# Four chained residual blocks on one core: adapter halves in fp16 turned by DMA, inner rows in one product, stacked low-rank product

## What is computed

```
x += attention with 16 heads: queries from f, keys and values from x, one own key and value per query from f,
     a length mask (always all-true here), projections Wq, Wk, Wv, Wo
x += softmax((x + stage embedding) @ f^T) @ f
x += layernorm(h + relu(h @ W1 + b1) @ W2 + b2) * gamma + beta     with h = x; W1 512x128, W2 128x512 of the batch's language
x += (x @ A^T) @ B^T + lang_embed                                  with A 16x512, B 512x16 of the batch's second language
```

## Time and profile before

| | us |
|---|---|
| median of 3 runs | 1315.94 (1315.02 to 1317.57) |
| the profiled execution: its time, its span | 1315.8, 1314.0 |
| PE busy | 1254.3 |
| DVE busy, ACT busy, POOL busy | 855.0, 849.9, 488.6 |
| one middle (batch 2 to 3), start to the next attention | 87.73 |

### The profile page before, as it was taken

The page is one execution under the profiler, slowest core; times in us unless marked ns, Lnnn a source line. Parts: engine busy times, 40 slices in busy tenths (PEclk is TensorE's granted clock), DMA queues, the critical chain, the costliest instruction groups (busy, mean ns, idle before and its releaser), DMA issues.

```text
span 1314.0 us, 19231 instructions
## 1 busy us (share of the span) xinstructions
PE 1254.3 (95%) x6697; PEld 519.7 (40%) x6697; DVE 855.0 (65%) x1553; ACT 849.9 (65%) x1803; POOL 488.6 (37%) x428
## 2 busy tenths in 40 slices
PE   7889999999999999999999999999999999999995
PEld 4332454325543345323543245431454324533252
DVE  5876449764596547964379643887439854497544
ACT  4898339873598636975379753888429883498631
POOL 6414363143731246321562416514254143631114
PEclk9999999999999999999999999999999999999997
DMA  6303532135223153132521334213343036222010
GB/s 217 69 13 107 113 65 65 54 97 103 57 57 92 64 97 73 41 123 51 91 61 49 115 73 81 63 44 107 89 78 74 19 107 121 57 65 68 25 33 32
DMA packets 156142, 98.85 MB, mean 75 GB/s; under 512 B 107338, under 2 KB 130182, under 8 KB 156046
## 3 DMA queue, kind: packets, MB, share of 16 engines
q1 hardware_dynamic: 155984, 97.61, 30.5%
q10 hardware_dynamic: 62, 0.01, 0.0%
HBM read 40.81 MB, written 8.40 MB: 37 GB/s over the span
## 4 chain that ended last, share of the span: by engine, by line
PE 66%; DVE 17%; ACT 14%; issue 2%; POOL 1%; ACTq 0%; POOLq 0%
PE bank L469 24%; PE banks L469 13%; DVE nmx L1086 10%; ACT big L858 7%; PE bank L1444 7%; PE banks L1428 6%; ACT banks L807 4%; PE banks L1363 4%; PE bank L1265 2%; PE bank L1391 2%; PE bank L1396 2%; PE bank L1418 2%; PE bank L1454 1%; DVE x L1147 1%; DVE big L1143 1%
## 5 line engine op out<-in xcount | busy, mean ns | idle before, releaser
L807 ACT ACTIVATE banks<-banks,nmx 128x512 f32<-128x512 f32 x512 | 342.4, 687 | 28.4 <-DVE nmx L1086 26.2
L1086 DVE TENSOR_REDUCE nmx<-banks 128x1 f32<-128x512 f32 x512 | 329.5, 685 | 35.8 <-PE banks L1363 34.7
L858 ACT ACTIVATE big<-banks 128x1024 f32<-128x1024 f32 x256 | 247.2, 1022 | 44.1 <-PE banks L1428 43.1
L469 PE MATMUL bank<-fT,w_hi 128*128 128x512 f16 x768 | 256.7, 380 | 0.7 <-DVE fT L1000 0.6
L1363 PE MATMUL banks<-KQ 97*128 97x512 f16 x512 | 196.5, 384 | 16.9 <-ACT banks L807 15.8
L1428 PE MATMUL banks<-KQ 98*128 98x512 f16 x512 | 141.0, 382 | 13.6 <-ACT big L858 8.7
L469 PE MATMUL bank<-fT,w_lo 128*128 128x512 f16 x384 | 145.9, 380 | 0.0
L504 POOL TENSOR_TENSOR split<-tiles_in,ones 128x512 f16<-128x512 f32 x56 | 60.3, 1078 | 223.5 <-DMA xT<-split 208.6
L504 POOL TENSOR_TENSOR half<-qk,ones 128x512 f16<-128x512 f32 x64 | 66.9, 1045 | 190.0 <-ACT qk L789 178.5
L1444 PE MATMUL bank<-big,V 128*32 128x512 f32 x1024 | 136.4, 605 | 0.0
L579 POOL TENSOR_TENSOR x<-x,bo_rows 128x512 f32<-128x512 f32 x32 | 40.0, 1280 | 236.7 <-DMA x<-in_x_dram 236.7
(11 more groups left out here) (153 smaller groups left out, 1813.2 us busy)
## 6 DMA issues: line engine op xcount, KB each, us to landing
KQ<-half SPq DMA_DIRECT2D x384, 64.0 KB, 2.0
tiles_in<-in_x_dram SPq DMA_DIRECT2D x32, 256.0 KB, 7.2
x<-in_x_dram SPq DMA_DIRECT2D x8, 1024.0 KB, 5.8
out_dram<-x SPq DMA_DIRECT2D x32, 256.0 KB, 2.0
tiles_in<-in_fside_BxSxS_dram SPq DMA_DIRECT2D x28, 256.0 KB, 3.5
w<-in_L_cond_W_dram SPq DMA_DIRECT2D x16, 256.0 KB, 4.7
b2r<-in_L_cond_b_dram SPq DMA_DIRECT2D x8, 256.0 KB, 4.5
gr<-in_L_cond_gamma_dram SPq DMA_DIRECT2D x8, 256.0 KB, 5.5
```

The source lines that it names most:

```text
L469: mm = eng.matmul(out_ap, pairs[n][0], pairs[n][1], start=(first and n == 0), stop=(last and n == len(pairs) - 1))
L807: eng.activation(bank(step, i)[:, v, :], bank(step, i)[:, v, :], ACT.Exp, bias=nmx[:, t, h:h + 1], accum_out=esum[:, t, h:h + 1]).then_inc ...
L858: eng.activation(big[:, n % 2, 2 * u:2 * u + 2, :], bank(step)[:, :, :], ACT.Exp).then_inc(read(step), 1)
L1086: eng.tensor_reduce(nmx[:, t, h:h + 1], bank(step, i)[:, v, :], AX_X, ALU.max, negate=True).then_inc(max_done, 1)
```

## The change

In the seven middles that have a next batch:

- X2T and X3T go. Instead ACT and DVE make the halves of each tile of x behind the second block (step X2, ahead of the first projection; POOL adds b2 there), and SP turns them by DMA into `aT2` (four turns, behind fT's). Behind SCALE, POOL makes the halves (step X3: `split`), and SP turns them (step T3).
- HID is one step for all 512 tokens: 12 fp16 products of 512 columns. LOW is one step for 256 tokens: eight fp16 products of 256 columns on rows stacked from halves of A, then a copy by ACT and a subtraction by DVE. LORA is one fp16 product with stacked halves. ADP stays fp32.
- NORM is done once for four tiles. POOL splits W1 once per batch (three more operations, `split_w1`).
- Groups of maxima open 24 slots behind Q. The last projection V 3 leaves its last three parts (six matmuls) to the attention, behind its first score products, and DVE takes it out of PSUM.
- The small tables are made by DVE in the middle of the attention; one DMA of the language row is moved to the parameters.

In the last batch X2T and X3T stay as PE transposes, but ACT takes the high half and DVE the low one.

```diff
-        n0, n2 = ([("NORM", t, n) for n in range(NORM_PIECES)] for t in (0, 2))
-        adapters = [("X2T", 0), None, ("HID", 0), None, ("ADP", 0), None, ("X2T", 1), ("SQ", 0), ("HID", 1), ("ADP", 1),
-                    ("SQ", 1), n0[0], ("X2T", 2), n0[1], ("HID", 2), n0[2], ("X2T", 3), n0[3], ("HID", 3), n0[4],
-                    n0[5], None, ("SCALE", 0), None, ("SCALE", 1), ("X3T", 0), None, ("LOW", 0), None, ("ADP", 2),
-                    None, ("ADP", 3), ("SQ", 2), ("LORA", 0), ("SQ", 3), ("X3T", 1), n2[0], ("LOW", 1), n2[1],
-                    n2[2], ("LORA", 1), n2[3], n2[4], n2[5], ("SCALE", 2), None, ("SCALE", 3), ("X3T", 2), None,
-                    ("LOW", 2), None, ("LORA", 2), ("X3T", 3), None, ("LOW", 3), None, ("LORA", 3)]
-    if not head:
-        return [step for step in adapters if step]
+
+        at = {13: [("HID", 0)], 15: [("ADP", 0)], 16: [("SQ", 0), ("ADP", 1)], 17: [("SQ", 1), ("ADP", 2)],
+              18: [("SQ", 2), ("ADP", 3)], 19: [("SQ", 3)], 26: [("SCALE", 0), ("X3", 0)], 28: [("SCALE", 1), ("X3", 1)],
+              30: [("T3", 0)], 31: [("T3", 1)], 32: [("SCALE", 2), ("X3", 2)], 34: [("SCALE", 3), ("X3", 3)],
+              38: [("LOW", 0), ("T3", 2)], 39: [("LORA", 0), ("T3", 3)], 40: [("LORA", 1)], 49: [("LOW", 1)],
+              50: [("LORA", 2)], 51: [("LORA", 3)]}
+        at.update({20 + n: [("NORM", 0, n)] for n in range(NORM_PIECES)})
+        adapters = [at.get(n, []) for n in range(max(at) + 1)]
...
+    slots = slots[:-LATE_PARTS]
+
+    opens = [slots.index(("Q", g)) + OPEN[tail][g] for g in range(NG)]
     maxima = [("SMAX", g, u, v) for g in range(NG) for u in range(2 * NT) for v in range(2)]
-    out, later = [], {}
+    out, later = [("X2", t) for t in range(NT) if tail], {}
...
+OPEN = ((32, 26, 26, 26), (24, 24, 24, 24))
 F16_AFTER = 12
 PARTS = 6
+
+LATE_PARTS = 3
...
+def tokens(step, head):
+
+    n = 1 if not head else NT if step[0] == "HID" else NT // 2
+    return slice(step[1] * n * P, (step[1] + 1) * n * P)
...
+                    elif step[0] == "X3":
+                        t = step[1]
+                        eng.wait_ge(x3_done, i * NT + t + 1)
+                        if t == 0:
+                            eng.wait_ge(x2t_in, i * NT * 16 + NT * 16)
+                        split(p16[:, t, 0:S], p16[:, t, S:2 * S], x1[:, t, :], x3_hi, i * NT + t + 1, x3_lo)
+
+            def split_w1(i):
+
+                eng.wait_ge(w1_in, i * 16 + 16)
+                eng.tensor_tensor(hT[:, :], hT[:, :], wide[:, 0:1].to_broadcast([P, S]), ALU.mult).then_inc(w1_wide, 1)
+                eng.wait_ge(w1_wide, i + 1)
+                halves = w1[:].rearrange("p h d n -> p h (d n)")
+                split(halves[:, 0], halves[:, 1], hT[:, :], w1_hi, i + 1, w1_lo)
...
+                    elif step[0] == "X2":
+                        t = step[1]
+                        eng.wait_ge(x2_lo, i * NT + t + 1)
+                        turn(aT2, t, p16[:, t, :], x2t_in)
+                    elif step[0] == "T3":
+                        t = step[1]
+                        eng.wait_ge(x3_lo, i * NT + t + 1)
+                        turn(aT2, t, p16[:, t, :], x3t_in[t // 2])
...
+                    elif kind == "X2":
+                        t = step[1]
+                        wait_read(eng, ("PV1", t), i)
+                        eng.activation(p16[:, t, 0:S], x1[:, t, :], ACT.Copy).then_inc(x2_hi, 1)
...
+                        eng.wait_ge(x2_hi, i * NT + t + 1)
+                        eng.tensor_tensor(p16[:, t, S:2 * S], x1[:, t, :], p16[:, t, 0:S], ALU.subtract).then_inc(x2_lo, 1)
...
+                    elif kind == "LOW":
+                        at = tokens(step, head)
+                        eng.wait_ge(low_hi, i * 2 + step[1] + 1)
+                        eng.scalar_tensor_tensor(out=lowT[LR:2 * LR, at], in0=bank(step, i)[LR:2 * LR, 0:at.stop - at.start],
+                                                 scalar=1.0 / WS, in1=lowT[LR:2 * LR, at], op0=ALU.mult, op1=ALU.subtract
+                                                 ).then_inc(read(step, i), 1)
...
+            def take_last_v(i):
+                step = ("V", NT - 1)
+                wait_full(eng, step, i)
+                eng.tensor_scalar(V[:, NT - 1, :], bank(step, i)[:, :], 1.0 / WS, None, ALU.mult).then_inc(read(step, i), 1)
...
                         transpose4(step, x1[:, t, :], i)
                     elif kind == "HID":
+                        at = tokens(step, head)
+                        if step[1] == 0:
+                            eng.wait_ge(w1_lo, i + 1)
+                            eng.wait_ge(par_in, i * 80 + 80)
+                        if head:
+                            eng.wait_ge(x2t_in, i * NT * 16 + NT * 16)
+                        else:
+                            wait_read(eng, ("X2T", step[1]), i)
+                        wait_free(eng, step, i)
+                        hi_lo(eng, bank(step, i)[:, 0:at.stop - at.start], [(w1[:, 0, d, :], w1[:, 1, d, :]) for d in range(ND)],
+                              [(aT2[:, 0, d, at], aT2[:, 1, d, at]) for d in range(ND)]).then_inc(done(step, i), 1)
...
+                        if head:
+                            eng.wait_ge(x3t_in[step[1]], i * 32 + 32)
+                        else:
+                            wait_read(eng, ("X3T", step[1]), i)
+                        wait_free(eng, step, i)
+                        for d in range(ND):
+                            for h in range(2):
+                                rows = a16[:, h, d, :, :].rearrange("p c r -> p (c r)")
+                                mm = eng.matmul(bank(step, i)[0:3 * LR, 0:at.stop - at.start], rows, aT2[:, h, d, at],
+                                                start=(d == h == 0), stop=(d == ND - 1 and h == 1))
+                        mm.then_inc(done(step, i), 1)
...
+                        eng.matmul(bank(step, i)[:, :], lowT[0:LOW_ROWS, t * P:(t + 1) * P], lowB[0:LOW_ROWS, :],
+                                   start=True, stop=True).then_inc(done(step, i), 1)
...
+                for part in range(PARTS - LATE_PARTS, PARTS):
+                    mm = project(("V", NT - 1), part, i)
+                mm.then_inc(done(("V", NT - 1), i), 1)
```

More of the change, by code:

```diff
@@ L120, in order_mid @@
         if adapters and i % 2 == 0:
-            out += [a for a in (adapters.pop(0),) if a]
+            out += adapters.pop(0)
         if rows and not sums and i >= late and not adapters:
@@ L132, in order_mid @@
     assert rows and i >= max(later)
-    return out + [a for a in adapters if a] + ([] if sums else [("SROW",)])
-OPEN = (32, 26, 26, 26)
+    return out + [a for each in adapters for a in each] + ([] if sums else [("SROW",)])
+OPEN = ((32, 26, 26, 26), (24, 24, 24, 24))
 F16_AFTER = 12
 PARTS = 6
+LATE_PARTS = 3
 WEIGHTS_AT = {("IN", 5): (1, 0), ("IN", 7): (0, 1), ("K", 0): (1, 1), ("Q", 1): (2, 1), ("K", 2): (3, 1)}
@@ L207, in order_last @@
                ("LORA", 2), ("LOW", 3), ("LORA", 3)])
-ADAPTER_STEPS = set(order_mid(True, False))
+ADAPTERS = ("X2", "X2T", "HID", "ADP", "SQ", "NORM", "SCALE", "X3", "T3", "X3T", "LOW", "LORA")
+def tokens(step, head):
+    n = 1 if not head else NT if step[0] == "HID" else NT // 2
+    return slice(step[1] * n * P, (step[1] + 1) * n * P)
 def plan_banks():
@@ L237, in plan_banks @@
             for step in order_mid(True, True):
-                give(step, i if step in ADAPTER_STEPS else i + 1)
+                give(step, i if step[0] in ADAPTERS else i + 1)
     return home, where
@@ L429, in build_program @@
         copied = sem("copied")
-        emb_in = sem("emb_in")
+        a_hi = sem("a_hi")
+        b_hi = sem("b_hi")
+        w1_in = sem("w1_in")
+        w1_wide = sem("w1_wide")
+        w1_hi = sem("w1_hi")
+        w1_lo = sem("w1_lo")
+        x2_hi = sem("x2_hi")
+        x2_lo = sem("x2_lo")
+        x2t_in = sem("x2t_in")
+        x3_hi = sem("x3_hi")
+        x3_lo = sem("x3_lo")
+        x3t_in = [sem(f"x3t_in{n}") for n in range(2)]
+        low_hi = sem("low_hi")
         par_in = sem("par_in")
@@ L589, in _ @@
             add_bo(B - 1)
-            mid(True, False, B - 1, [step for step in order_last() if step in ADAPTER_STEPS])
+            split_w1(B - 1)
+            mid(True, False, B - 1, [step for step in order_last() if step[0] in ADAPTERS])
         @block.sync
@@ L1146, in mid @@
                         wait_full(eng, step, i)
-                        eng.tensor_tensor(x1[:, t, :], bank(step, i)[:, :], x1[:, t, :], ALU.add
-                                          ).then_inc(read(step, i), 1)
+                        eng.scalar_tensor_tensor(out=x1[:, t, :], in0=bank(step, i)[:, :], scalar=1.0 / WS, in1=x1[:, t, :],
+                                                 op0=ALU.mult, op1=ALU.add).then_inc(read(step, i), 1)
             def take_norms(g, i):
@@ L1182, in attention @@
                     take_norms(g, i)
-                for g in range(1, NG):
```

(24 more changed lines are left out.)

220 lines of the change are left out of this document (118 added, 102 removed).

## The result

The changed kernel takes 1344.81 us (median of 4 runs, 1343.45 to 1345.53), the kernel before beside it 1315.48 (4 runs, 1314.99 to 1317.57). The ratio is 1.0219, with a 95% interval of 1.0201 to 1.0236: it is slower by 2.2%. Forecast was 1287, with a range of 1260 to 1310: the measured time lies outside it, and on the other side of no change.

A forecast was written before the change was run, and what follows sets the result against it. PE bounds the kernel, with DVE and ACT nearly as busy among the maxima. From 1315.8 us, seven middles save 31.5 and the first 1, the last batch adds 3: 1286.3, stated as 1287, range 1260 to 1310.

The forecast's parts named there:

- Group 0 of the maxima: Slots 35 to 52 of a middle: PE needs 12.4 us, DVE 15.8, so PE waits some 2.
- group 1: The second group of maxima in a middle: PE needs 11.6 us, with no wait added.
- The gate at group 3: PE waits 1.9 us at group 3's first maximum for the stack from POOL's chain, landing at 63.3.
- LOW and LORA: In groups 2 and 3, LORA waits some 1.2 us for ACT and DVE to read LOW; the next LORA 0.3.
- PE's own work: PE's work in a middle falls by 8.0 us, to 75.3: adapters 6.7 less, V 3's matmuls 1.3.
- Ahead of the maxima: The middle's opening stretch takes 21.0 us against 26.46, plus 0.2 for fT.
- The turns of x: Four DMA turns ahead of HID land at 491.0, at worst 492.7, before HID at 494: hidden.
- V 3's six matmuls: Moved behind the attention's first score products, where PE waits anyway: cost nothing there, 1.3 us without that cover.
- The last batch: Its row of dependent steps gets longer: +3 us, between +1 and +5.
- The DMA turns block for block: Turns ahead of HID take 42 us, holding PE up some 30 us a batch: near 1500 us; chance 1 in 100.
- The slower one: Rival: POOL's operations before group 3's stack take longer; no gain from 1.47 each, 1333 us at 1.6; chance 0.08.
- the third: Rival: gain mostly eaten by LORA's longer wait or DVE holding up maxima; 0.7 to 3 a middle, 1313 to 1297; chance 0.15.

The follow-up runs named there:

- hold: The changed kernel, with POOL's first SCALE waiting until DVE has normalised all four tiles: 1341.67 us, ratio 1.0195.
- spread: The changed kernel, with the four normalisings set apart in DVE's order, with maxima between them: 1328.66 us, ratio 1.0094.
- halfwait: loralate, with POOL's halving of Q2 at its old place in the order but waiting for the last small NORM operation: 1302.12 us, ratio 0.9881.
- poolload: loralate, with four more POOL multiplications in each middle, behind the seventh small NORM operation: 1325.75 us, ratio 1.0064.
- fill: The changed kernel, with sixteen useless matmuls in PE's order ahead of its long wait: 1331.68 us, ratio 1.0123.
- loralate: stackfirst, with the LORA products one entry (two slots) later: 1314.79 us, ratio 0.9994.
- stackfirst: spread, with SCALE and X3 of tiles 2 and 3 two entries later, behind the halves of K3 and Q3: 1323.08 us, ratio 1.0054.
- fillwait: loralate, with five and three useless matmuls meant for PE's two waits in group 1, which ran behind them: 1321.06 us, ratio 1.0032.

## Why the prediction was wrong

**The step that failed** is the price of DVE in "Group 0 of the maxima": "five pieces of NORM at 0.46, and four normalisings at 0.45 to 0.5", and "so PE waits some 2 us". Those durations were read from the earlier trace rows, and POOL stood idle beside them, for 12.45 us up to 546.52. In the changed kernel the same operations stand beside POOL's halving of Q2 and POOL's own SCALE, which the first normalised tile sets off. The four took 3.79 for 1.9, and two small operations beside the halving of Q2 took 1.0 for 0.17. The text put the fall of POOL's idle time into the forecast of the stack and left DVE at its quiet price, though "but what remains stands in one place" names the pile.

The place was wrong too. Group 0 took the 2 us of waits that the sum gave it (14.57 for 14.4), but the four normalisings, which the sum counts there, came only 2.5 us into group 1. There the sum had no wait at all: 20.37 for 11.6. Of these 8.8 us, 1.38 + 4.08 are waits, and 6.10 x (1 - 0.53) = 2.9 is the lower clock. The runs say what is behind each. Hold takes the meeting of POOL and the normalisings away, and 4.08 becomes 2.18; what is left is the pile by itself, and spread, which takes it apart, leaves 0.82. Halfwait takes the small operations out of POOL's way, and the 1.38 is gone. Poolload puts the meeting back elsewhere, and group 0 grows. Fill keeps the clock up and gives back 13 us in all, 1.9 a middle.

The kernel before had the collision in its trace, outside the rows that the prediction read. Three of the 34 small operations took 1.0 to 1.2 in each middle, ahead of the maxima, where PE was full and DVE had time to lose. DVE and POOL there:

```profile
498.44 1.00 DVE L1039 TENSOR_TENSOR st<-st 128x2 f32<-128x2 f32 x1
```

```profile
498.38 1.04 POOL L504 TENSOR_TENSOR half<-qk,ones 128x512 f16<-128x512 f32 x1 [1.42 <-ACT qk L789]
```

The changed kernel has three slow ones in a middle as well. So the change did not make slow small operations; it moved them to where DVE is the limit, and set two of the four normalisings beside POOL.

The Trainium skill, "Trainium Architecture — The Big Picture", section "What this means for kernel authors", says that DVE and GpSimd share a port pair, which it calls "an exclusive lock (not a bandwidth split)". The rows agree: all 21 slow small operations of the changed kernel, and all 21 of the kernel before, end 0.02 to 0.03 us behind the end of an operation of POOL's. The prediction had weighed the Trainium skill's softer sentence, on contention, in "GPSIMD Engine Reference", section "Specifications", and applied it to POOL's time. It also kept only half of it: beside two SBUF inputs the sentence names "a 2-port perf mode", and the normalisings, which have one tensor input, were slow here too. By the rows the short instruction lost most: 0.17 became 1.00, while POOL's 1.27 became 1.50.

**The clock** was no term of the sum at all, since it is 1.00 all through the middle of before that was read. A wait that the change makes can cost more than itself: in the changed kernel the lower clock cost some 1.9 us a middle, by fill. It costs nothing where PE is not the limit, as in group 1 of loralate.

**The gate at group 3** was the forecast's reason for 83.2. In the changed kernel it isn't there: POOL is done with Q3's halves 58.8 us into the middle, later than the 54.7 of the forecast, but PE comes still later. It is no phantom. It appears as soon as the pile is smaller, with 1.0 to 2.2 in hold and 0.8 to 1.9 in spread, and putting the halves ahead of SCALE took it away.

**LOW and LORA**: forecast 1.2 and 0.3 a pair; measured 0.65 and 0.35 in group 2, 1.29 and 0.35 in group 3: right in sum, 2.6 for 3.0. MROW's wait is 0.86 for 0.4, and 0.66 more is spent on an exponential in group 3.

**PE's own work** was right. In a middle of halfwait of 86.20 us PE is busy for 79.44 at a clock of 1.00; the last matmul ahead of each of its 16 waits counts 0.16 beyond its pace, which leaves 76.9, for 75.7 in the forecast's stages. The middle of before gives 84.7 in the same way (85.69 busy, six waits), so 7.8 of the forecast's 8.0 are there. In the changed kernel, whose middle is 4.5 longer than before's, the waits and the lower clock took 12.3; in halfwait, whose middle is 1.5 shorter, about 6.

**Small terms.** Ahead of the maxima 21.55 for 21.2. PE waits for fT in four of the seven middles, 0.21 to 0.65, which is the sum's 0.2 on average. (The text lets fT's last turn begin 4.8 before SP is done; its 485.6 is right, but follows from a turn that begins 1.34 before that.) The turns of x are hidden: no HID waits for a DMA. V 3's six matmuls cost nothing that shows in the attention: it and the second block take 70.4 to 71.6 us in place of 70.7 to 71.0. The start gains 2.2 for 1, but nearly 1 of it is luck: in the first middle of before's trace the clock over group 0 is 0.89, and 1.00 in the changed kernel's. The last batch costs 1.5 for +3, inside its 1 to 5. The DMA turns block for block, 1 in 100, did not come.

**The rivals.** The slower one (0.08) had the right engine and the wrong victim: it priced POOL's operations longer, at the stack, from 1.47 each on. They took 1.04 to 1.5 (only one of them over 1.33), and it was DVE that paid. The nearest to what happened is a clause of the third, "lets the maxima behind it stand", for a different cause and at 0.7 to 3 us in place of 8.8. A chance of 0.09 for slower was too low for a change that sets DVE's work of two places in one and gives POOL 95 us more of it (584 busy for 489).

## What to carry to other kernels

A duration of VectorE from a trace holds for the neighbour it had on GpSimd. Read its slowest rows in the same trace too: here they stood at 1.0 and 1.2 beside a usual 0.15, and told of the collision before the change was made. Where a change brings SBUF work of the two together, price each short VectorE operation by the end of the GpSimd operation that it can meet, and look at what queues behind it on VectorE. When such a pile is found, move the meeting, not the work: a wait of GpSimd's of some 1.5 us gave 12.7 us here, and the change that had cost 2.2% then saved 1.2%. And read a wait of PE with the granted clock of the stretch behind it, in every repetition of the stage and not in one: several us at half speed can follow, and they cost time only where PE is the limit.

## What the runs showed of the hardware that was not expected

- VectorE's operations on SBUF, also one of 128x4 with a single tensor input, wait for the running GpSimd operation to end: 0.17 became 0.89 to 1.11, and 0.53 for a normalising became 0.75 to 1.62. VectorE's operations that read PSUM (0.60 for a maximum, 0.74 for an addition that reads SBUF too) and ScalarE's normalisings on SBUF (0.81 to 0.91) do not wait so.
- TensorE's granted clock fell behind an idle time of 4.08 us in all seven middles of the changed kernel. Behind 1.38 and 0.82, with 2.3 us between their ends, it fell in one of seven middles of loralate, in two of fillwait (in one of them behind a third wait of 0.83) and in three of stackfirst, and stayed at 1.00 in the others; behind 0.92, 1.08, 0.82 and 0.82 in poolload it never fell. So the same waits in one and the same execution do not always give the same clock: what else decides was not settled.
- Left open too: the last 15 us between 1302 and the forecast. In the middle of halfwait counted above stand 14 waits of 0.2 to 0.7 us, most for an exponential, and in group 1 DVE is busy for all of its 13.85 us. No run took these away.
